# Three chained transformer-like blocks on one core: the opening's loads, setup steps and second adapter in another order

## The reference, cut to what matters

```
x = L0(x)   # adapter: gelu(x @ down), per sequence a 64x64 domain matrix, @ up, + x, layer norm
x = L1(x)   # adaptive layer norm, 16-head attention with bias and mask, feed-forward
x = L2(x)   # rotation of the features by two angles per sequence
x = L3(x)   # layer norm, instance norm with a style per subject, top-2 of 8 experts, + x

# L0
hidden = gelu(einsum('bsd,ad->bsa', x, down_W) + down_b)
domain_output = where(valid, einsum('bsa,boa->bso', hidden, expert_W[idx]) + expert_b[idx], hidden)
hidden = domain_output + domain_emb[idx]
x = layer_norm(einsum('bsa,da->bsd', hidden, up_W) + up_b + x)
# L1, its beginning
scale, shift = split(silu(sin_emb(timestep)) @ W_ada + b_ada)
x = ln(x) * (1 + scale) + shift
scores = (x @ Wq + bq)(x @ Wk + bk)^T / 4 + attention_bias, masked;  softmax;  @ (x @ Wv + bv)
# L3, its style
hyp = relu(se @ hyp_w1 + b) @ hyp_w2 + b;  sty = relu(hyp @ sty_w1 + b) @ sty_w2 + b
gamma, beta = split(sty);  gamma = softplus(gamma) + 1e-8
```

## Time and profile before

| what | value |
|---|---|
| runs | 699.59 us median of 3 (696.46 to 700.35) |
| profiled execution | 705.39 us, its span 703.6 us |
| mean granted TensorE clock | 0.891 |
| busy: PE, VectorE, ScalarE, GpSimd | 557.6, 474.8, 279.8, 257.8 us |
| domain numbers ready (end of L982) | 9.63 us |
| adapter norms of chunk 0 | 34.67 to 48.86 us |
| first projection | 55.23 us |
| residual behind the output projection of chunk 0 | ends at 111.70 us |

### The profile page before, as it was taken

How to read it: one execution, slowest core, us unless ns; L and a number is a source line. 1 busy time by engine, 2 the same in 40 slices (tenths; PEclk the granted TensorE clock), 3 DMA queues, 4 the chain that set the end, 5 groups by cost and what they waited for, 6 DMA issues and landing times.

```text
span 703.6 us, 15766 instructions
## 1 busy us (share of the span) xinstructions
PE 557.6 (79%) x5032; PEld 415.9 (59%) x5033; DVE 474.8 (67%) x1300; ACT 279.8 (40%) x576; POOL 257.8 (37%) x161
## 2 busy tenths in 40 slices
PE   2618577999678797765966589999889999999992
PEld 1505364666565484652755447767666777777771
DVE  5582798589979979862499772886553646565651
ACT  0314531634433325313443132566444535353540
POOL 0633554628406538022862050212441222222222
PEclk9558679999898899887988779999999999999997
DMA  8623465203115351306433684774432322222220
GB/s 289 226 89 120 152 203 192 68 1 121 59 62 189 142 177 63 120 32 241 178 120 121 246 295 179 285 270 75 123 92 43 53 34 47 33 48 36 49 42 0
DMA packets 41177, 86.50 MB, mean 123 GB/s; under 512 B 7321, under 2 KB 31810, under 8 KB 37026
## 3 DMA queue, kind: packets, MB, share of 16 engines
q1 hardware_dynamic: 22896, 65.16, 26.5%
q0 software_dynamic: 7200, 8.60, 7.2%
q10 hardware_dynamic: 11026, 12.02, 5.6%
HBM read 57.23 MB, written 29.44 MB: 123 GB/s over the span
## 4 chain that ended last, share of the span: by engine, by line
PE 51%; DVE 25%; issue 9%; ACT 5%; DMA 4%; ACTq 3%; POOL 2%; SPq 0%; another core or an unknown queue 0%; DVEq 0%; POOLq 0%
PE bank L1908 8%; PE bank L1733 6%; PE bank L1897 5%; PE bank L1899 4%; PE bank L1742 4%; PE bank L1898 4%; PE bank L1909 4%; PE bank L1630 2%; ACTq L845 2%; PE bank L1697 2%; DMA stage<-in_moe_w 2%; PE bank L1713 2%; PE bank L1687 2%; DVE stats L1028 2%; DVE w_moe L1153 2%
## 5 line engine op out<-in xcount | busy, mean ns | idle before, releaser
L1897 PE MATMUL bank<-xs_f,w_moe 128*128 128x128 f16 x624 | 123.3, 221 | 12.4 <-issue 6.5
L654 POOL DMA_INDIRECT out_x<-x_kept,ids x39 | 61.5, 1577 | 171.9 <-DVE x_kept L1499 120.0
L1899 PE MATMUL bank<-xs_f,w_moe 128*128 128x128 f16 x624 | 123.5, 221 | 0.5 <-issue 0.5
L1898 PE MATMUL bank<-xs_f,w_moe 128*128 128x128 f16 x624 | 122.8, 220 | 1.1 <-issue 1.1
L857 ACT ACTIVATE stage<-bank,cols 128x128 f32<-128x128 f32 x312 | 88.6, 376 | 83.3 <-PE bank L1899 34.0
L1897 PEld LDWEIGHTS bank<-xs_f,w_moe 128*128 x624 | 61.1, 98 | 49.6 <-issue 21.4
L1908 PE MATMUL bank<-w_moe,split 128*128 x208 | 79.2, 383 | 0.6
L606 POOL DMA_INDIRECT dispatched<-disp,slot x32 | 34.4, 1076 | 98.3 <-DVE disp L1253 56.2
L1733 PE MATMUL bank<-w_moe 128*128 128x512 f32 x128 | 60.7, 635 | 9.8 <-ACT w_moe L743 9.8
L1898 PEld LDWEIGHTS bank<-xs_f,w_moe 128*128 x624 | 61.4, 98 | 4.3 <-issue 1.5
L995 DVE SCALAR_TENSOR_TENSOR split<-stage,split 128x2048 f16<-128x2048 f32 x16 | 41.1, 2568 | 31.9 <-ACT split L693 31.9
(11 more groups left out here) (272 smaller groups left out, 1208.3 us busy)
## 6 DMA issues: line engine op xcount, KB each, us to landing
stage<-in_moe_w SPq DMA_DIRECT2D x16, 1024.0 KB, 7.9
w_split<-split SPq DMA_DIRECT2D x16, 1024.0 KB, 4.9
w_moe<-w_split SPq DMA_DIRECT2D x8, 2048.0 KB
w_moe<-in_bias SPq DMA_DIRECT2D x8, 1024.0 KB, 9.7
xs<-dispatched ACTq DMA_DIRECT2D x41, 130.0 KB
w_moe<-in_x_f SPq DMA_DIRECT2D x4, 512.0 KB, 5.6
w_moe<-in_x_t SPq DMA_DIRECT2D x4, 512.0 KB, 4.7
out_x<-x4b ACTq DMA_DIRECT2D x4, 512.0 KB
```

The source lines that it names most:

```text
L654: pool.indirect_dma_start(out=out[:, :], out_offset=bass.IndirectOffsetOnAxis(ap=ids[m][:, 0:1], axis=0), in_=ys[j], in_offset=None, bound ...
L1897: pe.matmul(o, hi, xs_f[j][:, k, :], start=(k == 0), stop=False)
L1898: pe.matmul(o, hi, xs_f[j][:, KD + k, :], start=False, stop=False)
L1899: mm = pe.matmul(o, lo, xs_f[j][:, k, :], start=False, stop=(k == KD - 1))
```

## The change

Nothing is computed otherwise; five engines' lists are put in another order.

- Loads: `ints` and `cols` alone stand first on SP; `domains` and `mats` go to ScalarE's queue ahead of `up_w` and `norm0`; `down_w` goes behind `x_f`. Each group has a semaphore of its own.
- The eight domain matrices of chunk 0 are issued four by SP and four by ScalarE, which reads the domain numbers too. `w_ada` and the style weights follow them, `w_qkv` and the rest come behind the Gelu and the sines.
- VectorE waits for `ints` and `cols` alone before the domain steps; the clearing of `v_bd` goes behind the angles; the adapter of chunk 0 goes ahead of `ada`, and the style steps behind `scale_norm(0)`. `split_low(0, 0)` stands before the first product's step, `split_low(0, 1)` behind the adapter residual of chunk 1 and the first `gamma3` steps.
- TensorE: the style products stand between the projections, `down_projection(1)` behind the values, `domain_experts(1)` between the halves of the scores, `up_projection(1)` behind them. Chunk 1's adapter has banks 6 and 7.
- GpSimd: `shift_norm(0)` before `mask(0)`.
- ScalarE: `split_high(0, 0)`, queries, keys, values and `hidden(1)` before Exp and Ln.

```diff
-ADAPTER_BANKS = ((2, 3, 2), (2, 3, 2), (7, 6, 6), (7, 6, 6))
+ADAPTER_BANKS = ((2, 3, 2), (6, 7, 6), (7, 6, 6), (7, 6, 6))
...
-        early = [
-            (ints, t["ints"]), (cols, t["cols"]), (domains, t["domains"]), (mats, t["mats"]),
-            (down_w, t["down_w"].rearrange("(k p) a -> p k a", p=P)),
-        ]
...
+        first = [(ints, t["ints"]), (cols, t["cols"])]
+        early = [(domains, t["domains"]), (mats, t["mats"])]
+        of_adapter = [(up_w, t["up_w"]), (norm0, t["norm0"].broadcast_to([P, 2, D]))]
+        of_style = [(subj_emb, t["subj_emb"]), (hyp_w1, t["hyp_w1"]), (sty_w2, t["sty_w2"])]
...
-            load_x(0)
+            load_features(0)
+            sp.dma_start(down_w[:], t["down_w"].rearrange("(k p) a -> p k a", p=P)).then_inc(down_in, 16)
+            load_experts(0, CB // 2)
+            load_tokens(0)
             load_bias(0)
...
-            mask(0)
             pool.wait_ge(cond_ready, 1)
             shift_norm(0)
+            mask(0)
             select(1)
...
+            act.wait_ge(dom_ready, 1)
+            _, chosen = nc.values_load_multi_w_load_instructions(
+                dom_at[0:1, CB // 2:CB], engines=[mybir.EngineType.Activation], min_val=0, max_val=NDOM - 1)
+            for b in range(CB // 2):
+                act.dma_start(w_raw[:, CB // 2 + b, :],
...
+            act.dma_start(w_ada[:], t["w_ada"].rearrange("(k p) n -> p k n", p=P)).then_inc(ada_in, 16)
+            for dst, src in of_style:
+                act.dma_start(dst[:], src).then_inc(style_in, 16)
 
             hidden(0)
...
+            act.dma_start(w_qkv[:], t["w_qkv"].rearrange("(k p) n -> p k n", p=P)).then_inc(qkv_in, 16)
+            for dst, src in main:
+                act.dma_start(dst[:], src).then_inc(main_in, 16)
+
+            split_high(0, 0)
+            queries(0)
+            keys(0)
+            values(0)
+            hidden(1)
             act.wait_ge(setup, SETUP_ABS)
...
+            hidden()
+            dve.wait_ge(adapter_in, N_ADAPTER)
+            residual()
+            norms()
+            dve.wait_ge(setup_pe, 2)
+            for m in range(2 * KD):
+                step(dve.tensor_scalar(ada[:, m, :], bank[5][:, B * m:B * m + B], b_ada[:, m:m + 1],
+                                       1.0 if m < KD else 0.0, ALU.add, ALU.add))
+            dve.drain().then_inc(cond_ready, 1)
+            scale_norm()
 
             step(dve.tensor_copy(sub_f[:], sub_i[:]))
             step(dve.tensor_scalar(sub_f[:], sub_f[:], 0.0, float(NSUB - 1), ALU.max, ALU.min))
             step(dve.tensor_scalar(hot_sub[:], sub_f[0:NSUB, :], iota_p[0:NSUB, 0:1], None, ALU.is_equal))
             assert done[0] == SETUP_SUB
...
+            split_low(0, 0)
+            dve.wait_ge(setup_pe, 3)
...
             assert done[0] == SETUP_ABS
+            values()
             dve.wait_ge(setup_act, 5)
             step(dve.tensor_scalar(soft[:, 2], soft[:, 1], 1.0, None, ALU.add))
+            scores(0)
+            hidden, adapter_residual, norms = adapter(1)
+            hidden()
+            scores(1)
+            adapter_residual()
...
-            split_low(0, 0)
-            values()
-            scores(0)
             split_low(0, 1)
-            scores(1)
-            hidden, adapter_residual, norms = adapter(1)
-            hidden()
             sums(0)
-            adapter_residual()
             sums(1)
             split_low(0, 2)
             norms()
...
+            project(0, 0, wq, q_done, range(0, 1))
+            pe.wait_ge(style_in, N_STYLE)
+            pe.wait_ge(setup, SETUP_SUB)
+            pe.matmul(bank[4][0:SE, 0:B], subj_emb[:], hot_sub[:], start=True, stop=True).then_inc(setup_pe, 1)
+            project(0, 0, wq, q_done, range(1, KD))
...
             values(0)
+            down_projection(1)
+            pe.wait_ge(setup, SETUP_SE + 3)
...
             scores(0, 0)
+            domain_experts(1)
             scores(0, 1)
-            pe.wait_ge(biased[1].sem, biased[1].of(0, 4))
-            down_projection(1)
-            domain_experts(1)
             up_projection(1)
-            pe.wait_ge(y_ready.sem, y_ready.of(1, 2))
             context(0, 0)
             context(0, 1)
+            pe.wait_ge(main_in, N_MAIN)
+            pe.wait_ge(y_ready.sem, y_ready.of(1, 2))
             output_projection(0)
```

More of the change, by code:

```diff
@@ L414, in build @@
         ]
-        N_EARLY, N_COND, N_MAIN = 16 * len(early), 16 * len(cond), 16 * len(main)
+        N_FIRST, N_EARLY, N_MAIN = 16 * len(first), 16 * len(early), 16 * len(main)
+        N_ADAPTER, N_STYLE = 16 * len(of_adapter), 16 * len(of_style)
         block = ctx.enter_context(nc.Block())
@@ L422, in _ @@
             sp.sem_inc(w_out.sem, 1)
-            for dst, src in early:
-                sp.dma_start(dst[:], src).then_inc(early_in, 16)
+            for dst, src in first:
+                sp.dma_start(dst[:], src).then_inc(first_in, 16)
             def load_features(c):
@@ L429, in load_features, with load_experts @@
                              ).then_inc(x_f_in.sem, 16)
-            def load_experts(c):
+            def load_experts(c, last=CB):
                 sp.wait_ge(dom_ready, 1)
@@ L434, in load_experts @@
                 _, chosen = nc.values_load_multi_w_load_instructions(
-                    dom_at[0:1, bass.ds(c * CB, CB)], engines=[mybir.EngineType.SP], min_val=0, max_val=NDOM - 1)
-                for b in range(CB):
+                    dom_at[0:1, bass.ds(c * CB, last)], engines=[mybir.EngineType.SP], min_val=0, max_val=NDOM - 1)
+                for b in range(last):
                     sp.dma_start(w_raw[:, b, :], t["exp_w"][bass.ds(chosen[b], 1), :, :].rearrange("e a o -> a (e o)")
@@ L772, in _ @@
             act.sem_inc(kept_ready.sem, 1)
[L773 to L776, removed]
+            for dst, src in early:
+                act.dma_start(dst[:], src).then_inc(early_in, 16)
+            for dst, src in of_adapter:
+                act.dma_start(dst[:], src).then_inc(adapter_in, 16)
             def store(c):
@@ L1329, in _ @@
             step(dve.tensor_scalar(gamma3[:], gamma3[:], 1e-8, None, ALU.add))
-            dve.wait_ge(setup_pe, 7)
-            for m in range(2 * KD):
-                step(dve.tensor_scalar(ada[:, m, :], bank[5][:, B * m:B * m + B], b_ada[:, m:m + 1],
-                                       1.0 if m < KD else 0.0, ALU.add, ALU.add))
-            dve.drain().then_inc(cond_ready, 1)
-            hidden()
-            residual()
-            norms()
-            scale_norm()
-            dve.wait_ge(main_in, N_MAIN)
-            split_low(0, 0)
-            values()
-            scores(0)
             split_low(0, 1)
-            scores(1)
-            hidden, adapter_residual, norms = adapter(1)
-            hidden()
             sums(0)
-            adapter_residual()
             sums(1)
@@ L1625, in turn1, with project @@
                     turn(xn1, k, TURN1_BANK[c], turn1_done)
-            def project(c, first_bank, w, done):
-                for m in range(KD):
+            def project(c, first_bank, w, done, parts=range(KD)):
+                for m in parts:
                     for k in range(KD):
```

104 lines of the change are left out of this document (49 added, 55 removed).

## The result

The changed kernel took 693.59 us (median of 9 runs; eight lie between 689.66 and 695.4), the kernel before 698.55 beside it (9 runs, 696.46 to 700.35). The remaining run of the changed kernel took 1877.85 us; it is in no ratio, and nothing on record explains it. The ratio is 0.9915, with a 95% interval of 0.9895 to 0.9935: 5.9 us faster (4.5 to 7.3). The forecast was 690.4 and 9.2 us; the time lies inside the range, the gain is two thirds of the forecast.

The account below looks back on a forecast made before the run. The bound was taken to be a chain of waits, almost only through VectorE, to the output residual. Its end moves from 111.70 to 102.4, less 0.1: 9.2 us off the median 699.59 gives 690.4, range 687 to 694.

Parts of the forecast that it names:

- Part 1: Opening up to the adapter's residual: earlier domain numbers and matrices end it at 22.5, not 34.67; gain 12.1 us.
- Part 2: Norms of chunk 0: with mask(0) behind shift_norm(0) they take 12.3 us, 1.9 less, ending at 34.8; total gain 14.0.
- Part 3: shift_norm(0) on GpSimd: the first split comes behind it, so the first projection starts at 39.5; gain 15.7 us.
- Part 4: Style products and down projection put between projections and scores: maximum at 63.6, not 73.88; gain falls to 10.3 us.
- Part 5, VectorE's branch: Second adapter beside the scores: split_low(0, 2) waits 5.5 us for its weight part, starts at 86.5; residual at 102.4.
- The other branch: Sums, probabilities, contexts and output projection: done at 99, 2 us before the norms end, so no bound.
- A: ScalarE's queue in the opening stalls again, Gelu moves from 13.7 to 19.4: 694.8 us; chance 0.14.
- B: Weight part lands in 5.5 us, gamma3 not blocked: norms end at 96.3, TensorE's branch binds, 687.5 us; chance 0.12.
- C: VectorE's fixed order puts split_low(0, 1) and weight part 2 behind delayed style round trips: 702 us; chance 0.08.
- D: Opening's gain is lost before the scores because w_qkv, issued later, lands last: 699 us; chance 0.08.
- Sum: At the output projection's residual: 111.70 to 102.4 is 9.3 us, less 0.1 for turn1(1), so 9.2 us gained.
- the tail: From chunk 0's first score maximum to the start of the output residual's second half; 39.4 us in the kernel before.

Follow-up runs that it names:

- third set of runs: The changed kernel against the kernel before, on another chip where the kernel before took 708.38 us: ratio 0.997 (0.9946 to 0.9995).

## Why the prediction was right or wrong

- **Part 1**: held, in part by errors that cancel. `dom_at` was ready at 5.36 (4.3 forecast), since `cols` took 3.40 us to land (2.3). Reading four numbers took 1.8 us (2.5), and the use came 1.65 behind the last issue (2.1): matrices used at 11.56 (11.5), residual's end 22.48 (22.5).
- **Part 2**: held. Norms from 22.51 to the end at 34.74, 12.2 us (12.3). The mask's price was 2.7 and not 1.9, since three steps would have waited and not two. Beside the moved mask the three steps for `sub_f` and `hot_sub` and the first split did wait (0.58, 0.96, 1.18 and 3.30 us), inside the slack that the prediction gave them.
- **Part 3**: held, 39.09 (39.5).
- **Part 4**: held, the last style group ends at 56.17 (55.6), the maximum at 64.15 (63.6). Other executions of the same kernel take up to 1.6 us longer over this stretch (last section).
- **Part 5, VectorE's branch**: held. `gamma3` waited 2.44 us for GpSimd, `split_low(0, 1)` ended at 77.49 (76.2), the stall before `split_low(0, 2)` was 4.4 (5.5), and it started at 87.01 (86.5). The norms ended at 101.6 (about 101).
- **Part 5, "The other branch ... 99, 2 us before the norms end, no bound"**: this step failed. TensorE's branch ended at 106, 7 us later, and set the end. I had copied 12.8 us from the kernel before as one block. That block begins with the second context's probabilities at 98.2, where the first context was long under way. Counted from the first context's start the same rows give 19.2 us, and with my own 82.5 for that start (78.9 and 3.62) the branch would have ended at 101.7, behind the norms. It started 1.3 later, at 83.83, and took 2.9 longer, since `split_high(0, 2)` is ahead of both contexts on ScalarE, which I had priced only for VectorE's split: 105.9. With that split behind the contexts the block is 18.9. The prediction follows the orders of GpSimd, SP and VectorE to the end; ScalarE's it does not follow past the split.
- **Rivals**: A did not come, since ScalarE's 7.99 us stop lies behind Gelu and is covered (the queries' copy comes at 42.87). The mechanism behind B was half seen: TensorE's branch did bind, but by being late and not by VectorE's being early. C's round trips of the style cost nothing, since TensorE ran without a gap from 39.09 to 56.17. But the order of VectorE that C names does cost, on TensorE's branch: the sums stand behind `gamma3` and `split_low(0, 1)`. D did not come: the first projection was released by `shift_norm(0)`.
- **Sum**: the first maximum starts at 61.86 and not at 71.58, a gain of 9.7 (10.3); the tail gives back 4.6 of it (1.1): 5.1 at the residual (9.2), 5.9 by the ratio. That the time still lies in the stated range of 687 to 694, at its upper edge, is partly luck: the branch that set the end is in the sum only as no bound, and the kernel before came out 1.0 us below the 699.59 that the sum starts from.

## What to carry to other kernels

Where a branch of the old kernel is called "no bound", take it apart again in the new order, engine by engine, and do not carry a block's length over: what overlapped its beginning may be gone. Follow a wait that is put ahead on an in-order engine to everything queued behind it; two such waits in parallel hide one another (0.6 and 2.7 us alone, 6.3 together), so take both away before judging either. Before work is moved between two stages, try the first half of a change alone: here the opening gave all, and the second adapter gained (about 1.6 us) only once the order around it was made for it.

## What the runs showed of the hardware

**The clock can fall in a wait of under 3 us, and need not.** At full clock TensorE idled 2.61 us and ran its next eight transposes in 1.97 us and not 1.09. Ahead of chunk 1's projections it idled 2.63 us in one kernel and started them at a granted clock of 0.50 (110 to 112 us, 8.62 us in all), and 2.68 us in another and started them at 1.00 (7.13 us). What decides is not shown. The same changed kernel takes 22.8 us from the first projection to the first maximum in one profile and 24.4 in another; the granted clock from 39 to 44 us is 1.00 in the first and 0.50 in the second. So the tail is compared here, and not the time of a first maximum.

**Holds at VectorE's `x4b` step.** In some profiles VectorE stops ahead of this step or the next while GpSimd issues its indirect transfers (`DMA_INDIRECT`, about 1 us each), though TensorE's products had ended. The same changed kernel has them in one profile (span 705.1) and not in another (690.1). Chains of waits, with and then without:

```profile
210.52 1.38 DVE w_moe L1047 x4
211.90 3.34 another core or an unknown queue
...
215.29 1.29 DVE x4b L1276 x2
216.58 2.95 another core or an unknown queue
```

```profile
211.77 1.05 DVE w_moe L1047 x3
212.83 1.20 DVE x4b L1276 x2
214.03 0.58 DVE w_moe L1058
```

The chain has two more such gaps, 5.73 us ahead of `x4b` at 313.28, and 2.96 us on TensorE at 512.87. The four come to 15.0 us, as much as the spans differ, but the match is loose: at the second chunk's `x4b` three of them (12.0 us) are passed, and that profile is only 8.3 us behind. All seven profiles from the two chips where the kernel before takes 708 us have such holds, and none of the five from the chip where it takes 699. The profiled execution before has one too (5.71 us at 314.31), as large as the 5.8 us by which it lies above the median. So they differ between executions of one and the same kernel, and are not this change's. Whether they are why the ratio was 0.997 in the third set of runs is not shown, since no profile of the kernel before was taken beside it. What causes them was not tried and stays open.
